# Sparse hidden layer: gate rounds of two tiles on alternating banks, and comparisons written in a row

## The reference

```python
inter = xf @ c1_w.T @ c2_w.T
blk = inter.reshape(B * T, n_blocks, SPARSITY)
idx = jnp.argmax(blk, axis=-1) + jnp.arange(0, INTER, SPARSITY)
w1_g = w1[idx]
w2_g = w2t[idx]
h = jax.nn.relu(jnp.einsum('bkm,bm->bk', w1_g, xf))
out = jnp.einsum('bk,bkm->bm', h, w2_g)
```

## Time and profile before

| | |
|---|---|
| median of three runs | 3545.76 us |
| the profiled execution's own time | 3546.57 us |
| its span, first to last instruction | 3544.9 us |
| TensorE products busy | 3365.6 us (95%) |
| VectorE busy | 2272.8 us (64%) |
| ScalarE busy | 1576.9 us (44%) |
| GpSimd busy | 1065.9 us (30%) |
| granted TensorE clock, mean | 0.98 |
| Sign activations, L1800, x728 | 223.1 us busy, mean 761 ns |

### The profile page before, as it was taken

The page is one execution under the profiler, slowest core; times in us unless marked ns, Lnnn a source line. Parts: engine busy times, 40 slices in busy tenths (PEclk is TensorE's granted clock), DMA queues, the critical chain, the costliest instruction groups (busy, mean ns, idle before and its releaser), DMA issues. The chain is left out here.

```text
span 3544.9 us, 52710 instructions
## 1 busy us (share of the span) xinstructions
PE 3365.6 (95%) x18226; PEld 2996.3 (85%) x18226; DVE 2272.8 (64%) x3815; ACT 1576.9 (44%) x3332; POOL 1065.9 (30%) x1220
## 2 busy tenths in 40 slices
PE   6999999799999899999999899999978999999998
PEld 4888888699999899999999778688768988978777
DVE  5555567676766577777777533333247888867876
ACT  4333344343433577777777422322265555521220
POOL 0000000000000577777776100000013555536554
PEclk8999999899999999999999999999989999999999
DMA  3333332354444434443432644544335777789888
GB/s 118 107 97 104 97 106 84 99 142 123 117 120 120 113 99 113 113 113 109 113 97 77 200 125 121 172 131 123 115 124 200 256 272 264 258 303 353 285 286 312
DMA packets 490422, 556.80 MB, mean 157 GB/s; under 512 B 174276, under 2 KB 370372, under 8 KB 490212
## 3 DMA queue, kind: packets, MB, share of 16 engines
q1 hardware_dynamic: 438308, 368.12, 35.4%
q0 software_dynamic: 50848, 183.92, 15.0%
q10 hardware_dynamic: 1056, 2.10, 0.2%
HBM read 440.86 MB, written 113.18 MB: 156 GB/s over the span
## 5 line engine op out<-in xcount | busy, mean ns | idle before, releaser
L2194 PE MATMUL wo_acc<-wo_w,wo_l 128*128 128x512 f32 (+1 forms) x2496 | 576.3, 393 | 21.0 <-DVE wo_l L2144 20.8
L269 PE MATMUL kv_bank<-kv_wo,kv_so 128*128 128x512 f32 x2436 | 573.8, 394 | 16.4 <-DVE kv_wo L361 11.0
L2194 PEld LDWEIGHTS wo_acc<-wo_w,wo_l 128*128 128x128 f32 (+1 forms) x2496 | 461.2, 185 | 135.9 <-DVE wo_w L2168 20.4
L269 PEld LDWEIGHTS kv_bank<-kv_wo,kv_so 128*128 128x128 f32 x2436 | 457.3, 190 | 110.9 <-issue 17.4
L657 PE MATMUL pr_bank<-pr_xo,pr_wp 128*128 128x400 f32 x2688 | 498.6, 347 | 29.0 <-ACT pr_s L724 13.4
L657 PEld LDWEIGHTS pr_bank<-pr_xo,pr_wp 128*128 128x128 f32 x2688 | 493.4, 190 | 31.8 <-DVE pr_wp L741 24.0
L1725 PE MATMUL hid_acc<-x1t,hid_w 128*128 128x304 f32 x2688 | 411.7, 310 | 0.1
L2469 PE MATMUL w_acc<-w_w,w_l 128*128 128x512 f32 (+1 forms) x1680 | 386.3, 393 | 9.8 <-DVE w_l L2418 5.8
L1725 PEld LDWEIGHTS hid_acc<-x1t,hid_w 128*128 128x128 f32 x2688 | 391.2, 195 | 1.3 <-DVE hid_w L1848 0.3
L2469 PEld LDWEIGHTS w_acc<-w_w,w_l 128*128 128x128 f32 (+1 forms) x1680 | 309.4, 184 | 86.4 <-DVE w_l L2418 5.9
L2144 DVE TENSOR_TENSOR wo_l<-wo_l_raw,wo_l 128x512 fp32r<-128x512 f32 (+1 forms) x208 | 139.2, 671 | 341.7 <-ACT wo_l L2117 341.5
(11 more groups left out here) (210 smaller groups left out, 5011.0 us busy)
## 6 DMA issues: line engine op xcount, KB each, us to landing
wo_l_raw<-o_scratch SPq DMA_DIRECT2D x192, 256.0 KB, 2.9
pair_raw<-in_L_xattn_Wq_dram SPq DMA_DIRECT2D x64, 512.0 KB, 5.9
q_scratch<-pr_out SPq DMA_DIRECT2D x128, 200.0 KB, 2.6
o_scratch<-o_stage SPq DMA_DIRECT2D x64, 400.0 KB, 3.7
q_raw<-q_scratch SPq DMA_DIRECT2D x64, 384.0 KB, 3.2
stage<-in_ctx_dram SPq DMA_DIRECT2D x45, 512.0 KB, 3.8
h_scratch<-c_raw SPq DMA_DIRECT2D x28, 608.0 KB
wo_w_raw<-in_L_xattn_Wo_dram SPq DMA_DIRECT2D x16, 1024.0 KB, 7.4
```

Source lines behind the costliest of these rows:

```text
L269: last = pe.matmul(bank[:, BANK[i], :], so[:, i, a, c, :], wo[:, i, e, c, :], start=(not opened and c == 0 and (a, e) == PAIRS[0]), stop=( ...
L2194: last = pe.matmul(acc[p][:rows, :], l[j % 2][:, a, k, :rows], w[:, c, m * per + k, :], start=(m == 0 and k == 0 and (a, c) == PAIRS[0]), ...
```

## The change

Three things go together.

1. The gates of a pair are made in seven rounds of two tiles (the last of one). A round fills one of the two banks, which the rounds use by turns, the next pair beginning with the other. So a round waits for the comparisons of the round before the last.
2. `equal` has tile and group outside and the 64 positions inside, so that an activation writes its 64 results in a row. The key operation reads them at a step of 128 elements (256 bytes) and writes a new tensor `ranked` in the old order; it is no longer in place. `halved` and `quartered` write to the mask's memory in place of buffers of their own.
3. The order is written anew. TensorE makes rounds 0 and 1 after tile 0, then one round after each of the next five tiles; the last comes before tile 2 of block 1. Of VectorE's row steps (one by one, as cut by `ends`) 1, 2, 3 and 2 come in the four tiles of block 0, none and 2 in the first two of block 1, 1 after the second tree and the rest, 3, at the end; no row step stands inside a tree. The first tree follows round 5, the second follows round 6 and two row steps.

The arithmetic is the same.

```diff
-    picks = [(a, min(4, tt - a)) for a in range(0, tt, 4)]
+    picks = [(a, min(2, tt - a)) for a in range(0, tt, 2)]
     NP = len(picks)
-    assert NP == 4
+    assert NP == 7
+    in_half = (4, 3)
+    after = ((0, 1), (2,), (3,), (4,), (5,), (6,), (), ())
...
-        equal = [sb(f"equal{x}", [P, pair, sparsity, g], BF16) for x, g in enumerate(spans)]
+        equal = [sb(f"equal{x}", [P, g, pair, sparsity], BF16) for x, g in enumerate(spans)]
+        ranked = [sb(f"ranked{x}", [P, pair, sparsity, g], BF16) for x, g in enumerate(spans)]
...
-        half = sb("half", [P, pair, sparsity // 2, most], BF16)
-        quarter = sb("quarter", [P, pair, sparsity // 4, most], BF16)
...
-            pool.sem_inc(compared, 1)
...
-            def gates(i, k):
+            def gates(i, m, k):
...
-                pe.wait_ge(compared, NP * i + k + 1)
-                pe.sem_inc(waited, 1)
+                if not isinstance(i, int) or i > 0 or k > 1:
+                    pe.wait_ge(compared, NP * i + k - 1)
+                    pe.sem_inc(waited, 1)
                 for x in range(n):
-                    last = pe.matmul(gate[:, x // 2, (x % 2) * 2 * P:(x % 2 + 1) * 2 * P],
+                    last = pe.matmul(gate[:, (m + k) % 2, x * 2 * P:(x + 1) * 2 * P],
...
+                    for t in range(tiles):
+                        sums(j, p, t)
+                        if (p, t) == (0, 0):
+
+                            pe.wait_ge(masked, 2 * (i + 1))
+                        close(m, p, t)
+                        if another and t < 2:
+                            turn_w(i + p, 1 - p, t)
+                        if late:
+                            for k in ((2, 3), (4,), (5, 6), ())[t]:
+                                gates(1, 1, k)
+                        elif more:
+                            for k in after[4 * p + t]:
+                                gates(i + 1, 1 - m, k)
...
                 for x in range(n * per):
-                    last = act.activation(equal[x_half][:, x % pair, :, at + x // pair], values[:, x, :], ACT.Sign,
+                    last = act.activation(equal[x_half][:, at + x // pair, x % pair, :], values[:, x, :], ACT.Sign,
                                           bias=top[:, a * per + x:a * per + x + 1])
...
+                    for t in range(tiles):
+                        evacuate(i, p, t)
+                        if another and t < 2:
+                            high_part(j + 1, 1 - p, t)
...
+                        elif more:
+                            for k in after[4 * p + t]:
+                                signs(i + 1, 1 - m, k)
...
-                dve.wait_ge(compared, NP * i + 2 * x + 3)
-                dve.tensor_tensor(equal[x][:, :, :, :], equal[x][:, :, :, :], key_bf[:, :, :spans[x]].rearrange(
+                dve.wait_ge(compared, NP * i + sum(in_half[:x + 1]))
+                dve.tensor_tensor(ranked[x][:, :, :, :], equal[x][:, :, :, :].rearrange("q a b c -> q b c a"), key_bf[:, :, :spans[x]].rearrange(
                     "q (b c) a -> q b c a", b=1).to_broadcast([P, pair, sparsity, spans[x]]), ALU.add).then_inc(step, 1)
...
-                dve.tensor_tensor(half[:, :, :, :g], equal[x][:, :, :n, :], equal[x][:, :, n:, :], ALU.max).then_inc(step, 1)
+                dve.tensor_tensor(mask[m][x][:, :, :n, :], ranked[x][:, :, :n, :], ranked[x][:, :, n:, :], ALU.max).then_inc(step, 1)
...
             def first_pair():
-                for x in range(2):
-                    largest(0, 2 * x)
-                    largest(0, 2 * x + 1)
-                    tree(0, 0, x, ())
+                for k in range(4):
+                    largest(0, 0, k)
                 low_part(1, 1, 0)
                 low_part(1, 1, 1)
...
+                largest(0, 0, 4)
+                largest(0, 0, 5)
+                tree(0, 0, 0, ())
+                largest(0, 0, 6)
+                tree(0, 0, 1, ())
...
-                cuts = (0, 2, 4, 9, 10, 10, len(mine)) if more else (0, 3, 6, 9, 12, 15, len(mine))
-                a, b, c, d, e, f = [mine[cuts[n]:cuts[n + 1]] for n in range(6)]
+                ends = (1, 3, 6, 8, 8, 10, 11, len(mine)) if more else (2, 4, 6, 8, 10, 12, 14, len(mine))
+                part = [mine[a:b] for a, b in zip((0,) + ends, ends)]
...
+                for x in range(8):
+                    if x < 2:
+                        low_part(2 * i + 1, 1, x)
+                    if more:
+                        if x in (4, 5):
+                            low_part(2 * i + 2, 0, x - 4)
+                        for k in after[x]:
+                            largest(i + 1, 1 - m, k)
+                        if x == 4:
+                            tree(i + 1, 1 - m, 0, ())
+                        if x == 6:
+                            tree(i + 1, 1 - m, 1, ())
+                    steps(part[x])
```

More of the change, by code:

```diff
@@ L1576, in hidden_layer @@
     per = 2 * P // sparsity
-    picks = [(a, min(4, tt - a)) for a in range(0, tt, 4)]
+    picks = [(a, min(2, tt - a)) for a in range(0, tt, 2)]
     NP = len(picks)
-    assert NP == 4
+    assert NP == 7
+    in_half = (4, 3)
+    after = ((0, 1), (2,), (3,), (4,), (5,), (6,), (), ())
     pair = per // 2
-    spans = [sum(n for _, n in picks[2 * x:2 * x + 2]) * 2 for x in range(2)]
+    spans = [sum(n for _, n in some) * 2 for some in (picks[:in_half[0]], picks[in_half[0]:])]
     most = max(spans)
@@ L1736, in body @@
                     if early:
+                        gates(0, 0, 0)
+                        gates(0, 0, 1)
                         for t in range(tiles):
-                            gates(0, t)
                             sums(j, p, t)
-                        turn_w(0, 1, 0)
-                        turn_w(0, 1, 1)
+                            gates(0, 0, t + 2)
+                            if t == 1:
+                                turn_w(0, 1, 0)
+                                turn_w(0, 1, 1)
+                        gates(0, 0, 6)
                         pe.wait_ge(masked, 2)
@@ L1744, in body @@
                             close(m, p, t)
-                        gates(1, 0)
+                        gates(1, 1, 0)
+                        gates(1, 1, 1)
                         continue
[L1747 to L1769, removed]
+                    for t in range(tiles):
[11 more added lines that the diff above has]
+                                gates(i + 1, 1 - m, k)
             turn_w(0, 0, 0)
@@ L1810, in body @@
                     if early:
-                        for k in range(NP):
-                            signs(0, k)
+                        for k in range(4):
+                            signs(0, 0, k)
+                        high_part(1, 1, 0)
+                        high_part(1, 1, 1)
+                        for k in range(4, NP):
+                            signs(0, 0, k)
+                        for t in range(tiles):
+                            evacuate(i, p, t)
+                        signs(1, 1, 0)
+                        signs(1, 1, 1)
+                        continue
                     if another:
                         act.wait_ge(summed, tiles * (j + 1))
[L1816 to L1826, removed]
-                        high_part(j + 1, 1 - p, 0)
-                    if more and not late:
-                        signs(i + 1, 2 * p)
-                    evacuate(i, p, 1)
-                    if late:
-                        signs(1, 2)
-                    if another:
-                        high_part(j + 1, 1 - p, 1)
-                    evacuate(i, p, 2)
-                    if more:
-                        signs(i + 1, 2 * p + 1)
-                    evacuate(i, p, 3)
+                    for t in range(tiles):
+                        evacuate(i, p, t)
+                        if another and t < 2:
+                            high_part(j + 1, 1 - p, t)
+                        if late:
+                            for k in ((2, 3), (4,), (5, 6), ())[t]:
+                                signs(1, 1, k)
+                        elif more:
+                            for k in after[4 * p + t]:
+                                signs(i + 1, 1 - m, k)
             high_part(0, 0, 0)
```

64 lines of the change are left out of this document (24 added, 40 removed).

## The result

The changed kernel takes 3593.84 us (median of 4 runs, 3587.58 to 3599.08), the kernel before 3547.85 on the same chips: ratio 1.0126, 95% interval 1.0113 to 1.0139. That is 46 us slower, where +27 was forecast. The profiled execution took 3587.58 us, its span 3585.9; it is the fastest of the four. The hidden layer, from its first turn of w1 to its last closing, takes 579.8 us in it (2600.0 to 3179.8) and 533.6 before (2606.2 to 3139.8): 46.2 more. The last stage is as it was (401.0 us from its first product, 399.3 before). So the time came in where the prediction looked.

What follows compares the result with a forecast made beforehand. TensorE was taken as the bound, with gaps. Ten pairs' +28, early pairs' +1.6 and +0.5, and -3.3 in the second pair made +27 on 3546.57, median 3573 us; range 3530 to 3596.

Steps and rivals of the forecast that it cites:

- three signs: Forecast wrong if key operation takes under 2.7 us, gate wait is missing, or row steps wait longer for gathers.
- Key operation: VectorE's read at a 256-byte step: 1.82 ns an element, 3.9 and 2.5 us, 4.3 more a pair.
- Rival 1: Key operation's step costs only the lost pairing, 1.04 ns an element: -9, 3537 us; chance 0.24.
- Comparisons: ScalarE's writes in a row start 0.21 us apart; eight take 1.8 us, where sixteen took 4.7.
- Rival 3: ScalarE's comparisons stay 0.28 us apart because the write isn't their limit: +52, 3598 us; chance 0.06.
- Gate round 2: TensorE waits for comparisons until 7.9 us after the mask, a new wait of 2.8 us a pair.
- The next weights: ScalarE's copy of 0.60 us, followed by VectorE's low part, done 21.8 us after the mask.
- the walk: One pair traced from mask ready: 38.3 us after the change, 35.5 before, so 2.8 lost a pair.
- constant 1.1: Old pair's 36.6 us measured less 35.5 walked, for a late row (0.50) and slow products; added again after the change.
- ten pairs: The steady pairs of the hidden layer lose 2.8 us each, 28 in all.
- second pair: Rounds of two tiles with faster comparisons give back 3.3 us near the layer's start.
- Rival 4: Row steps fall better than walked and the gate wait of 2.8 halves: +13, 3559 us; chance 0.12.

Runs made afterwards that it cites:

- the probe: Additions, reductions and comparisons at several steps timed alone, with none of the kernel computed; an addition element costs 0.53 ns in a row, 1.77 to 1.80 at 16 to 32 bytes.
- cheap gathers: Changed kernel with six ring slots in place of five and, after the first six, gathers of a quarter row each: 3575.02 us, ratio 1.0069.
- straight read: Changed kernel with the key operation reading comparisons in memory order, so keys meet the wrong comparisons: 3537.10 us, ratio 0.9966.
- the old order: Kernel before, with its four rounds and own order, given only the new comparison layout and key operation: 3598.34 us, ratio 1.0143.
- mask wait moved: Changed kernel with TensorE's mask wait and tile 0's closing put behind tile 1's products: 3596.03 us; the same edit on the kernel before: 3541.51 us.
- old-layout run: Changed kernel's seven rounds and new order, with comparisons laid out and key operation in place as before the change: 3540.36 us, ratio 0.9979.
- four kernels: Mask wait moved, the old order, and the changed kernel with row steps inside the trees (3606.21 us) or spread (3601.02 us); all 40.9 to 41.0 us a pair.

## Why the prediction was right, and where its size was off

The measured 3593.84 us lies in the stated range of 3530 to 3596, 2 us from its upper end, and outside the forecast's own 3563 to 3588. The direction and the cause, the key operation's read at a step, were right; the size was not, and that the range held it is partly luck: its upper end was set by doubts about other terms. Of the three signs that the prediction said would prove it wrong, one came (row steps wait longer for gathers) and one nearly did (the gate wait is 0.7 us a pair in place of 2.8).

- **Key operation**: forecast 3.9 and 2.5 us, measured 3.85 and 2.39. The bound chosen by the nearest row was the right one. The probe shows why it was near: reduction and addition pay the same for a step. The Trainium skill (Advanced Engine Details and Errata, SBUF Cachelines) has lines of 16 bytes that should be hit twice; the probe agrees, since the price rises between 8 bytes (1.05 ns) and 16 (1.77). Rival 1 goes by the rule of the Trainium skill (VectorE: DVE Perf Modes, The perf-mode tier table). With its 1.04 ns it would be right for steps of 2 and 4 elements and is not for this one.
- **Comparisons**: eight take 1.75 us (1.8 forecast), sixteen 3.39. Starts are about 0.20 apart. Durations still grow a little in a row, to 0.42 in the probe, which costs nothing. Rival 3 is out, although its 3598 is nearer to the result than the forecast's 3573.
- **Gate round 2**: 8.0 us behind the mask, 7.9 forecast. The wait of 2.8 us before it shows as 0.4 only: behind a mask wait of 3.77 the turn, the gates and the products at the lower clock take 1.09, 1.20 and 4.83 us in place of 0.64, 0.72 and 3.50, and fill most of it. The instant was right, its name in the view of waits wasn't.
- **The next weights**: copied at 21.2 us, before the low part at 21.8. Right to there.
- **The term that was too small** stands in the last sentence of the walk: "gathers follow VectorE with more slack". They have less. The prediction had named this as what would make it wrong ("if row steps wait for gathers longer than now"), and gave it no price; its walk left row arrivals out and put 0.5 us for them into a constant 1.1. Measured, the row ahead of the low part is 3.1 us late in the mean of ten pairs, against 1.0 before, and 2.9 of the 3.27 us at 2887.23 are on the path (without it the low part could start at 2885.47). So these waits grew by 2.1 us a pair; cheap gathers took 1.9 off the pair (40.85 - 38.94), and it had grown by 1.4 more than forecast.
- **Why the row is late** is not the long key operation by itself. Rows are as late in the run with the straight read (34.3 us of waits, 29.2 here), with a key operation of 1.2 us; and they are not late in the old order (0.6 us) or with the mask wait moved (0.8 us), with one of 3.9. GpSimd stood idle with all slots taken before the change too: 3.79 us at the place where it is 4.01 now (before 2877.80). What goes with the lateness is SP's load of the next weights. The sentence on the queues looked at their order, which did stay, and not at their distance. In the kernel before the load is issued 5.8 to 6.5 us behind the row's gather, and the row is usable 5.1 to 6.1 us after its issue. In the old-layout run it is mostly 3.1 behind and the row takes 6.0 to 6.8; in the ten pairs of the changed kernel and in about half of those of the straight read it is 2.4 behind, and the row takes 6.1 to 8.8. No run moves the load alone, so this is read from the traces and not shown by an experiment.
- **The rest of the sum**, measured in the two profiled executions:

| | forecast | measured |
|---|---|---|
| layer's first turn to first closing | +0.5 | +0.6 (37.2 against 36.6) |
| second pair | -3.3 | -2.9 (30.2 against 33.1) |
| the next two | +1.6 | +3.4 |
| ten pairs | +28 | +42.4 |
| last pair | 0 | +2.7 |
| sum | +27 | +46.2 |

- **The last pair** was called unchanged. Behind its mask wait of 3.85 us the first 24 products run at a granted clock of 0.50 (3151 to 3156); here the changed kernel, then the kernel before:

```profile
3151.07 5.83 PE L1726 MATMUL hid_acc<-x1t,hid_w 128*128 128x304 f32 x24
...
3113.34 3.58 PE L1725 MATMUL hid_acc<-x1t,hid_w 128*128 128x304 f32 x24
```

- **Rival 4** had the order in the other direction: the row steps fell worse, not better. In rival 1, "0.2 a pair" and "+2.7 in ten" don't agree by 0.7 us, which changes nothing.

What stays open: whether moving the weights' load away from the gather gives the time back, how much six slots with whole rows would give, and why four kernels share one length of a pair. No version with the turned read beats the kernel before. The two that do, each by 0.2%, keep the layout of before: seven rounds on it (3540.36), and the mask wait behind a tile (3541.51).

## What to carry to other kernels

Moving a strided access from a writer with slack to a reader on the path was a loss here, although the sum of both engines' busy time fell: ask which engine is in the loop. When the order or the length of a loop changes, walk its transfers too, with their distances and not only their order: a row whose step stands right ahead of work on the path needs a price of its own. And an experiment that moves work to remove a wait must say whether the new place is on the path: three of mine removed the late rows and hid the gain.

## What the runs showed of the hardware

- VectorE, bf16 addition of 1024: 0.69 us in a row, 1.22 at steps of 2 and 4 elements, 1.96 to 1.99 at 8 to 16, 1.88 turned over 64 or 128; with the output at step 4, 2.42, dearer than any read.
- ScalarE's comparisons of 64 start 0.197 us apart for outputs in a row and at steps of 2 and 4, with durations that grow to 0.42, 0.58 and 0.78 (the series follow one another without a pause, so each begins near where the last one ended); at step 8 or 10 they start 0.28 apart and last 1.18. The knee is at the same place as VectorE's.
- 24 products behind a wait of TensorE of 2.6 us took 5.05 us (cheap gathers; 3.91 behind another such wait in the same run), behind 3.8 us 4.83 (the changed kernel), behind 5.3 us 5.97 (mask wait moved), in place of 3.5; the granted clock is 0.50 there. The mean of 2676:3130 falls with it: 0.94 in the changed kernel, 0.91 with the mask wait moved, 0.98 before, and 1.00 with the mask wait moved on the kernel before, where no wait is over 1.5 us.
- A gathered row was usable 5.1 to 6.1 us after its issue where the load of the weights came 5.8 to 6.5 us behind it, and 6.1 to 8.8 where it came 2.4 behind. Gathers of quarter rows landed 3.0 us after their issue in the median, whole rows 6.4 to 7.2 in the old-layout run.
